# Output projection of a cross-attention stage in bursts, with the next layer's normalisation moved into it

## The reference, cut to what matters

```python
def _attend(q, k, v):                         # 16 heads of 64; once for 77 text keys, once for 179 image keys
    sim = jnp.einsum('bihd,bjhd->bhij', q, k) * SCALE
    attn = jax.nn.softmax(sim, axis=-1)
    out = jnp.einsum('bhij,bjhd->bihd', attn, v)
...
out = out + IMG_SCALE * out_ip
return out @ Wo + bo                          # 1024 -> 512: the output projection
...
def act_qdq(x):                               # in _L0_ffn_ref, on its input and on every intermediate tensor
    qmax = 2.0 ** (ACT_BITS - 1) - 1.0        # 32767
    scale = jnp.maximum(jnp.max(jnp.abs(x)) / qmax, 1e-12)
    return jnp.clip(jnp.round(x / scale), -qmax - 1.0, qmax) * scale
...
x = x + _L0_xattn_ref(_layernorm(x, axis=-1), ctx_1024, L0_xattn_Wq, ...)
x = x + _L0_ffn_ref(_layernorm(x, axis=-1), L0_ffn_w_gate, L0_ffn_w_up, L0_ffn_w_down)
```

## Time and profile before

| | us |
|---|---|
| median of the runs (lowest, highest) | 3874.53 (3872.53, 3882.94) |
| the profiled execution, its own time | 3887.41 |
| its span, first to last instruction | 3885.8 |
| TensorE busy | 3228.7 (83%) |
| VectorE, ScalarE, GpSimd busy | 2026.4, 1531.7, 709.6 |
| mean granted clock of TensorE | 0.915 |

### The profile page before, as it was taken

One profiled execution on the slowest core, in us unless ns is written; L12 is line 12 of the kernel. 1 busy time (PEld: TensorE's weight loads), 2 busy tenths in 40 slices (PEclk: granted clock), 3 DMA queues, 4 the chain that ended last, 5 costly groups with the idle time before them and its releaser, 6 DMA issues. The chain is left out here.

```text
span 3885.8 us, 52312 instructions
## 1 busy us (share of the span) xinstructions
PE 3228.7 (83%) x17152; PEld 2765.4 (71%) x17152; DVE 2026.4 (52%) x3424; ACT 1531.7 (39%) x2927; POOL 709.6 (18%) x1093
## 2 busy tenths in 40 slices
PE   7999799999999717998991069968881999999998
PEld 6989788888888606886880058836761877777776
DVE  3343377767677564556899955416763222222221
ACT  2222266666666423335777856503332111111110
POOL 0000277777777410000000000000000000000000
PEclk9999899999999858999995579978995999999999
DMA  6666544444444233445665544313324000100000
GB/s 173 170 206 188 176 141 140 134 130 140 137 139 124 78 103 133 160 141 171 210 205 165 164 140 162 135 57 109 120 89 121 22 33 33 33 30 31 20 31 16
DMA packets 330783, 457.31 MB, mean 118 GB/s; under 512 B 55616, under 2 KB 199232, under 8 KB 327946
## 3 DMA queue, kind: packets, MB, share of 16 engines
q1 hardware_dynamic: 316660, 438.94, 36.3%
q0 software_dynamic: 3328, 14.68, 1.0%
q10 hardware_dynamic: 10592, 1.04, 0.2%
HBM read 276.29 MB, written 144.70 MB: 108 GB/s over the span
## 5 line engine op out<-in xcount | busy, mean ns | idle before, releaser
L2254 DVE SCALAR_TENSOR_TENSOR lf_hT<-lf_hb,lf_hT 128x512 fp32r<-128x512 f32 x128 | 88.6, 692 | 638.4 <-ACT lf_hT L2312 637.1
L2312 ACT ACTIVATE lf_hT<-lf_hb 128x512 fp32r<-128x512 f32 x128 | 76.6, 599 | 699.2 <-PE lf_py L179 641.6
L177 PE MATMUL dn_py<-qf_wd,dn_om 128*128 128x512 f32 x384 | 150.5, 392 | 220.4 <-DVE dn_om L1641 220.4
L694 POOL TENSOR_TENSOR at_prob<-at_prob,at_rec 128x308 f32<-128x308 f32 (+1 forms) x256 | 261.5, 1044 | 230.8 <-DVE at_rec L731 230.8
L775 ACT ACTIVATE at_prob<-at_sc,at_nm 128x77 f32<-128x77 f32 (+1 forms) x1024 | 292.8, 381 | 3.7 <-DVE at_nm L718 3.6
L718 DVE TENSOR_REDUCE at_nm<-at_sc 128x4 f32<-128x308 f32 (+1 forms) x256 | 164.9, 686 | 178.4 <-PE at_sc L822 178.4
L177 PEld LDWEIGHTS dn_py<-qf_wd,dn_om 128*128 128x128 f32 x384 | 72.6, 189 | 235.8 <-issue 220.8
L788 ACT ACTIVATE at_pT<-at_tp 128x1024 fp32r<-128x1024 f32 x128 | 131.6, 1028 | 258.3 <-PE at_tp L832 258.2
L178 PE MATMUL lf_hb<-lf_xT,lf_w 128*128 128x512 f32 x512 | 203.7, 398 | 5.2 <-issue 5.2
L177 PE MATMUL lf_hb<-lf_xT,lf_w 128*128 128x512 f32 x512 | 205.1, 401 | 0.0
L179 PE MATMUL lf_hb<-lf_xT,lf_w 128*128 128x512 f32 x512 | 203.4, 397 | 0.0
(11 more groups left out here) (304 smaller groups left out, 9458.6 us busy)
## 6 DMA issues: line engine op xcount, KB each, us to landing
at_kr<-k_rows SPq DMA_DIRECT2D x256, 128.0 KB, 2.9
at_qs<-at_qst SPq DMA_DIRECT2D x512, 64.0 KB, 2.0
raw_gate<-pg_stage SPq DMA_DIRECT2D x96, 256.0 KB, 2.0
pu_rg<-raw_gate SPq DMA_DIRECT2D x96, 256.0 KB, 2.9
raw_up<-pu_stage SPq DMA_DIRECT2D x96, 256.0 KB, 2.0
om_raw<-raw_up SPq DMA_DIRECT2D x48, 512.0 KB, 3.8
dn_raw<-raw_up SPq DMA_DIRECT2D x48, 512.0 KB, 3.8
xn_parts<-pr_xturned SPq DMA_DIRECT2D x32, 512.0 KB, 3.8
```

The source lines that it names most:

```text
L177: pe.matmul(out, lh, rh, start=start, stop=False, **kw)
L694: ins = pool.tensor_tensor(prob[:, i, :, lo:hi], prob[:, i, :, lo:hi], rec[:, z, g, :].unsqueeze(2).broadcast_to([P, 2 * NTE, hi - lo]), A ...
L2254: dve.scalar_tensor_tensor(hT[:, i, 1, :], hb[i][:], 0.0, hT[:, i, 0, :].bitcast(F32), ALU.max, ALU.subtract).then_inc(h_done, 1)
```

## The change

- **Bursts.** `out_part` with its 4 pieces is replaced by `project_out`: all 24 matmuls of a tile at the end of one step in four (`out_tile(s)`, steps 12, 16, 20, ...). The buffers of the attention outputs grow from 10 to 13 pairs for it.
- **Normalisation in the pair stage.** For the tile projected in step s: VectorE adds it to the residual in step s+1, ahead of the second `totals`, and takes its statistics at the step's end; GpSimd makes the deviation and the shift at the start of step s+2; ScalarE normalises into `xn` in step s+3, ahead of `high_parts`; in step s+4 TensorE turns the tile in `pj` before its scores, ScalarE copies it out before its turned probabilities, VectorE takes the row maxima; in step s+5 SyncE stores it as float32 into `x1_turned`. The next `project_out` waits for `o_taken`, that copy.
- **Buffers and lags.** `place_values` works on pair s-3 instead of s-2 (`LAG_P` 2 to 3), in 2 buffers instead of 3 (`NVP`). The loops run 4 steps longer.
- **The pass is gone.** `normalize_all` and `normalized_rows` are deleted. The scale is worked out at the end of the pair stage. The gate projection loads the float32 rows (1 MB a chunk instead of 0.5 MB), ScalarE turns them into integers first and then makes the high part, and SyncE stores the integers to `xq` for the up projection.

The diff, cut to its core:

```diff
@@ attend_pairs
-    LAG_T, LAG_V, LEAD_Q, LAG_P = 3, 4, 3, 2
+    LAG_T, LAG_V, LEAD_Q, LAG_P = 3, 4, 3, 3
-    NPR, NY, NO, NQ, NQS, NK, NKR, NVP = 4, 3, 10, 4, 2, 4, 4, 3
-    OPIECES = 4
-    FIRST, LAST = -LEAD_Q, N + LAG_O
+    NPR, NY, NO, NQ, NQS, NK, NKR, NVP = 4, 3, 13, 4, 2, 4, 4, 2
+    EVERY = NPAIR // NTE
+    FIRST, LAST = -LEAD_Q, N + LAG_O + 4
...
-        def out_piece(s):
+        def out_tile(s):
             i = s - LAG_O
-            return (i // NPAIR, i % NPAIR // OPIECES, i % OPIECES) if 0 <= i < NPAIR * B else None
+            return (i // NPAIR, i % NPAIR // EVERY) if 0 <= i < NPAIR * B and i % EVERY == EVERY - 1 else None
@@ SyncE
+                def store_turned(b, t):
+                    n = NTE * b + t
+                    sp.wait_ge(o_taken, n + 1)
+                    lo = b % NB * S + t * P
+                    sp.dma_start(xt_d[b // NB].rearrange("p (k n) -> p k n", k=KD)[:, :, lo:lo + P], xt[:, n % 2]).then_inc(xt_stored[n % 2], 16)
...
-                    done = s - LAG_O - NPAIR - 1
+                    done = s - LAG_O - NPAIR - 3
...
+                    if out_tile(s - 5):
+                        store_turned(*out_tile(s - 5))
@@ GpSimd
+                def deviation(b, t):
+                    steps = Count(pool, norm_steps, 3 * (NTE * b + t))
+                    wait_alone(pool, mv_ready, NTE * b + t + 1, spacer_p)
+                    steps.done(pool.tensor_scalar(var[:], mv[:, 1:2], EPS, None, ALU.add))
+                    steps.wait()
+                    if b + t:
+                        pool.wait_ge(xn_ready, NTE * b + t)
+                    steps.done(pool.tensor_tensor(rstd[:], var[:], neghalf[:, 0:1], ALU.pow))
+                    steps.wait()
+                    steps.done(pool.tensor_tensor(shift[:], mv[:, 0:1], rstd[:], ALU.mult))
+                    wait_alone(pool, norm_steps, steps.base + steps.n, spacer_p)
+                    pool.tensor_scalar(shift[:], shift[:], -1.0, None, ALU.mult).then_inc(shift_ready, 1)
...
-                for s in range(-LEAD_KL, N + LAG_P):
+                for s in range(-LEAD_KL, LAST + 1):
+                    if out_tile(s - 2):
+                        deviation(*out_tile(s - 2))
                     if 0 <= s - LAG_P < N:
                         place_values(s - LAG_P, 0)
...
+                pool.wait_ge(row_max, 1)
+                pool.partition_all_reduce(big[:, 0:1], mx_row[:], P, RMAX).then_inc(all_max, 1)
@@ VectorE
+                def statistics(b, t):
+                    n = NTE * b + t
+                    dve.wait_ge(y_done, n + 1)
+                    dve.bn_stats(st[:], y[:, b % NY, t, :]).then_inc(stat_done, 1)
+                    wait_alone(dve, stat_done, n + 1, spacer_d)
+                    if n:
+                        dve.wait_ge(shift_ready, n)
+                    dve.bn_aggr(mv[:], st[:]).then_inc(mv_ready, 1)
+                def row_maximum(b, t):
+                    n = NTE * b + t
+                    dve.wait_ge(xn_ready, n + 1)
+                    dve.tensor_reduce(mx[:, n:n + 1], xn[:], AX_X, ALU.max, apply_absolute_value=True).then_inc(mx_done, 1)
...
                         totals(s - 1, 0)
+                    if out_tile(s - 4):
+                        row_maximum(*out_tile(s - 4))
                     if 0 <= s - LAG_T < N:
                         turned_low(s - LAG_T)
+                    if out_tile(s - 1):
+                        output(*out_tile(s - 1))
                     if 0 <= s - 1 < N:
                         totals(s - 1, 1)
                         reciprocals(s - 1)
                     if s < N + LAG_V:
                         low_parts(s)
-                    piece = out_piece(s - 1)
-                    if piece and piece[2] == OPIECES - 1:
-                        output(*piece[:2])
+                    if out_tile(s - 1):
+                        statistics(*out_tile(s - 1))
@@ ScalarE
+                def normalized(b, t):
+                    n = NTE * b + t
+                    wait_alone(act, shift_ready, n + 1, spacer_a)
+                    if n:
+                        act.wait_ge(o_full, n)
+                        act.wait_ge(mx_done, n)
+                    act.activation(xn[:], y[:, b % NY, t, :], ACT.Identity, bias=shift[:], scale=rstd[:]).then_inc(xn_ready, 1)
...
+                    if out_tile(s - 4):
+                        turned_output(*out_tile(s - 4))
                     if 0 <= s - LAG_T < N:
                         turned_high(s - LAG_T)
...
                         keys_high(s + LEAD_KH)
-                    high_parts(s)
+                    if out_tile(s - 3):
+                        normalized(*out_tile(s - 3))
+                    if s < N + LAG_V:
+                        high_parts(s)
@@ TensorE
+                def turn_output(b, t):
+                    pe.wait_ge(xn_ready, NTE * b + t + 1)
+                    for k in range(KD):
+                        ins = pe.transpose(pj[:, k * P:(k + 1) * P], xn[:, k * P:(k + 1) * P], ident[:])
+                    ins.then_inc(o_full, 1)
+                def project_out(b, t):
+                    if b + t:
+                        pe.wait_ge(o_taken, NTE * b + t)
+                    if t == 0:
+                        pe.wait_ge(vq_done, v_count(NPAIR * b + NPAIR - 1))
+                    for p in range(NPAIR):
...
+                    ins.then_inc(out_full, 1)
                 for s in range(FIRST, LAST + 1):
+                    if out_tile(s - 4):
+                        turn_output(*out_tile(s - 4))
...
-                    piece = out_piece(s)
-                    if piece:
-                        out_part(*piece)
+                    if out_tile(s):
+                        project_out(*out_tile(s))
@@ quantized_ffn
-                    normalize_all(nc, x1, xq, big, scal, ident, neghalf)
-                    project(nc, "pg", xq, wg, raw_gate, big, S_G, I_G, scal, meanwhile=lambda ph: Meanwhile(
+                    project(nc, "pg", xq, wg, raw_gate, big, S_G, I_G, scal, turned=xt_d, meanwhile=lambda ph: Meanwhile(
@@ project, ScalarE
                     act.wait_ge(xi_ready[par], 16 * half + 16)
+                    if turned is not None:
+                        act.wait_ge(x_lo, c + 1)
+                        act.wait_ge(xq_stored[par], 16 * half + 16)
+                        act.activation(xi[:, par], xf[:, par], ACT.Copy, scale=scal[:, I_X:I_X + 1]).then_inc(x_int, 1)
+                        act.wait_ge(x_int, c + 3)
```

More of the change, by code:

```diff
@@ L226, in cross_attention @@
         project_context(nc, a, x_in, ctx_in, xn_d, k_d, v_d, wq, wo, ident, neghalf)
[L227 removed]
+        attend_pairs(nc, a, x_in, xn_d, k_d, v_d, x1, xt_d, wq, wo, big, scal, ident, neghalf)
 def project_context(nc, a, x_in, ctx_in, xn_d, k_d, v_d, first, second, ident, neghalf):
@@ L538, in _, with attend_pairs @@
                         turn(n)
-def attend_pairs(nc, a, x_in, xn_d, k_d, v_d, x1, wq, wo, ident):
+def attend_pairs(nc, a, x_in, xn_d, k_d, v_d, x1, xt_d, wq, wo, big, scal, ident, neghalf):
     SEG = [(0, TEXT), (TEXT, S)]
@@ L573, in attend_pairs @@
         pj = ph.ps("pj", [P, D])
+        xn = ph.sb("xn", [P, D])
+        xt = ph.sb("xt", [P, 2, KD, P])
+        st = ph.sb("st", [P, 6])
+        mv = ph.sb("mv", [P, 2])
+        var = ph.sb("var", [P, 1])
+        rstd = ph.sb("rstd", [P, 1])
+        shift = ph.sb("shift", [P, 1])
+        mx = ph.sb("mx", [P, B * NTE])
+        mx_row = ph.sb("mx_row", [P, 1])
+        stat_done, mv_ready, norm_steps, shift_ready, xn_ready, mx_done, o_full, o_taken = (
+            ph.sem(n) for n in ("stat_done", "mv_ready", "norm_steps", "shift_ready", "xn_ready", "mx_done", "o_full", "o_taken"))
+        xt_stored = [ph.sem(f"xt_stored{i}") for i in range(2)]
+        row_max, all_max, settled, spacer_d, spacer_p, spacer_a = (
+            ph.sem(n) for n in ("row_max", "all_max", "settled", "spacer_d", "spacer_p", "spacer_a"))
         cleared, bo_ready = ph.sem("cleared"), ph.sem("bo_ready")
@@ L799, in high_parts @@
                     ins.then_inc(vq_hi, 1)
-                for s in range(FIRST, N + LAG_V):
+                for s in range(FIRST, LAST + 1):
+                    if out_tile(s - 4):
+                        turned_output(*out_tile(s - 4))
                     if 0 <= s - LAG_T < N:
@@ L1272, in project @@
-def project(nc, name, xq, w, raw, big, scale, inverse, scal, raw_gate=None, gate=None, meanwhile=None):
+def project(nc, name, xq, w, raw, big, scale, inverse, scal, raw_gate=None, gate=None, turned=None, meanwhile=None):
     NBANK = 4
@@ L1293, in project @@
         xi_ready = [ph.sem(f"xi_ready{i}") for i in range(2)]
-        x_hi, x_lo = ph.sem("x_hi"), ph.sem("x_lo")
+        x_int, x_hi, x_lo = ph.sem("x_int"), ph.sem("x_hi"), ph.sem("x_lo")
+        xq_stored = [ph.sem(f"xq_stored{i}") for i in range(2)]
         r_full, r_copied, max_done = ph.sem("r_full"), ph.sem("r_copied"), ph.sem("max_done")
```

(21 more changed lines are left out.)

159 lines of the change are left out of this document (21 added, 138 removed).

## The result

| | before | after |
|---|---|---|
| median of the runs (lowest, highest), us | 3878.31 (3872.53, 3882.94), 4 runs | 3817.47 (3811.49, 3821.6), 4 runs |
| the profiled execution, its own time | 3887.41 | 3818.55 |
| its span | 3885.8 | 3816.9 |
| mean granted clock of TensorE | 0.915 | 0.923 |

The ratio is 0.9837, 95% interval 0.9823 to 0.9852. The forecast was 3818 us. The median before now has a fourth run in it; the forecast started from 3874.5, the median of the first three, so it stood for 56 us less, where the medians differ by 61.

The account below looks back on a forecast made before the run. TensorE was taken to bound the pair stage and gate projection, the deleted stage being serial time. Removal -89, tiles +17, ends +16 gave -56 us, from 3874.5 to 3818 us; own range 3790 to 3840, overall 3775 to 3855.

Parts of the forecast that it names:

- The removal: Before the gate projection: the 90.5 us stage goes, first gate matmul near 1408.6 instead of 1497.49, -89 us.
- The tile: Pair stage, steps 13 to 125: 26.35 us without bias, 28.15 with; mean 27.9 against 27.3, +17 us.
- The four transposes: TensorE in the pair stage: four added transposes a tile, 4 x 0.099 = 0.40 us.
- The head and the last steps: Pair stage ends: first twelve steps +2 us, as the first bias delays the placing; light steps 125 to 127, -4.
- The tail: After the last scores: delayed placing 3.4, two more projection pieces 2.8, uncovered serial chain 8 and 3.5; +18 us.
- beside the last store: End of the pair stage: the maximum over rows and its reduction run beside the last store.
- The price of the power: GpSimd's deviation: the one-column power takes 0.41 us, between 0.20 and 1.04; the chain 1.45 us.
- Rival D: GpSimd's one-column power costs 1.04 us as before: +20 us, or +30 with the SP queue; 3843 us, chance 0.10.
- B: Pair stage: queues and slack absorb GpSimd's and VectorE's lateness, tile 24.7 + 0.36, 78 us less; 3740 us, chance 0.12.
- C: Gate projection: ScalarE's double conversion holds the banks, +27 us; 3845 us, chance 0.07.
- E: Pair stage: two or three half-clock stretches a tile; at 2.5 a tile +99 us, 3917 us; chance 0.05.
- One sign to look for: Pair stage, every second tile: TensorE waits at `at_vq` on GpSimd's `at_vs`, 2.5 to 3.5 us.

Follow-up runs that it names:

- e_bias4: Changed kernel with GpSimd adding the bias in step 4 of 8 (the burst step) instead of step 5; 3766.57 us.
- e_devlate: Changed kernel with GpSimd's deviation behind the placing of the values instead of ahead of it; 3790.6 us.
- e_bursts_lag3: Kernel before with the bursts alone, plus values placed for pair s-3 in 2 buffers; separate pass over x1 kept; 3829.13 us.
- e_bursts: Kernel before with only `project_out` in place of the four pieces, old lag of 2, separate pass over x1 kept; 3799.96 us.
- e_noreduce: Changed kernel with the reduction over partitions at the pair stage's end replaced by a plain GpSimd copy; 3822.21 us in one run.
- e_inburst: Changed kernel with bias, statistics, deviation and normalisation moved to the time of the next burst, transposes eight steps behind their own burst; 3734.43 us.
- before_again: Kernel before, unedited, run again for a second trace; 3875.8 us in one run.
- after_again: Changed kernel, unedited, run again for the spread and a second trace; 3817.78 us, ratio to before 0.9824.

## Why the prediction was right, and where it was not

**The removal.** Predicted -89 us. From the first dequantising instruction of VectorE to the first gate matmul it is 144.8 us before (1352.7 to 1497.5) and 55.9 after: -88.9. Conversion 2.00 for 1.91; the load issued at 1427.43 is used at 1432.23, 4.8 for 5.2. Right.

**The tile.** Without the bias 4.69 + 4.91 + 6.13 + 10.25 = 25.98 us, predicted 26.35. With it, at full clock, 28.44, predicted 28.15. Half-clock stretches came in nine of the 14 tiles with the bias and cost some 2.05 us where they came, which is 1.3 for each of the 14 and 0.66 for the mean tile; predicted 0.68, from nine in ten at 1.5 each. That these two agree is luck: they came less often than forecast and cost more. So is part of the rest: in the tile without the bias the forecast had 0.5 us for a wait of the transposes on ScalarE's normalisation, and the profile lists no such wait in 600:1200. The mean of the 28 tiles from step 13 to 125 is 27.87, predicted 27.9. The mechanism is shown too: e_bias4 takes the bias out of GpSimd's late step and the long wait is gone; e_devlate takes the deviation from ahead of the placing and the wait halves. In the forecast this term holds two things that run against each other: the bursts and the lag bring the tile from 27.39 to 25.39 (e_bursts_lag3), and the normalisation brings it back to 27.87. The sum against before came out at +13.5 instead of +17, since before's own tile over these steps was 27.39, while the forecast worked with 27.3.

The four transposes cost what the row said. In the tile without the bias the values start at 904.65 and take 2.95, and the transposes start behind them:

```profile
907.59 0.66 PE L944 MATMUL at_pj<-ident,at_xn 128*128 128x128 f32 x4
908.00 1.20 PE L908 MATMUL at_sc<-at_ks,at_qs 128*128 128x256 f32 x8
```

They put 0.41 us into the path. The figure of the Trainium skill ("TensorE: Matmul & The Clock Gate", Part 4), about 275 ns for one transpose of 128x128 in bf16, would by estimate give 1.1 us if each had to end before the next. As the time of one instruction the trace agrees with it, for float32: 273 ns is the median of the 128 at L944. But in a stream the next work starts some 0.1 us after each, and that is what they cost.

**The head and the last steps.** Predicted +2 and -4. The placing was late in step 7 as said (6.64 us instead of 4.70), but a wait on a DMA of 2.55 us with a half-clock stretch, in step 8 of before, did not come back: -3.2 from step 0 to 13. That is luck of this pair of profiles, and no effect of the change: in the second profile of the kernel before this wait is 1.05 us and no stretch follows, in e_bursts it is 3.44, and between the second profiles these steps differ by +1.8, as forecast. Steps 125 to 127: -6.

**The tail is the mis-sized term.** Predicted +18, measured +26.5 (+28.2 between the second profiles): from the last scores to the dequantisation it is 38.7 us before and 65.2 after. The chain between the last two bursts takes 5.7 us from the end of the addition (1352.57) to the next burst (1358.24), not 4.0, and stands in the path twice; the transposes take 1.11 at half clock, not 0.4; the last burst takes 7.50 us (1358.24 to 1365.74) and not the 5.6 of full clock. The prediction put the reduction "beside the last store". It starts 3.68 us after the row maximum that it reads has ended, and VectorE's wait of 4.09 for it stands there, but e_noreduce shows that only 0.8 us of it counts. The phase change behind the stage takes 10.6 us (1372.08 to 1382.70), where it took 8.8 before (1343.9 to 1352.7). Together 2 x 1.7 + 1.9 + 1.8 = 7.1 of the 8.5 us; the other 1.4 is not told apart. e_bursts_lag3, with 46.4 us for the same distance, puts 7.7 of the 26.5 on the bursts and the lag and 18.8 on the normalisation. The forecast counted the links of the tail at full clock, but TensorE is idle between them, and of the clock the transposes and the burst were granted this (columns as in the earlier trace rows):

```profile
1356.40:1358.20 1.80, 1.11 (x4) 0.71 (x4) 0.69 (x1) 0.60 (x1) 0.00 (x0) 0.50 0.00 0
1358.20:1365.80 7.60, 7.50 (x24) 5.71 (x24) 0.02 (x1) 0.00 (x0) 0.00 (x0) 0.75 0.12 35
```

The errors cancel: 13.5 - 3.2 - 6 + 26.5 = +31 in the stage, where the forecast had +17 + 16 = +33, so the stage and the removal give -58, for -56. Between the second profiles it is -50. So the mechanism of the tile and the removal was right, and the closeness of 3817.5 to 3818 is luck to some us. (The distance between the spans of the two profiles, 69, has 11 of the untouched stages in it.)

**The price of the power** on one column is 0.57 us, between the 0.41 chosen and the 1.04 of the earlier trace rows; the whole chain is 1.58, not 1.45. Rival D, which had it at 1.04, fell: 32 x 0.16 = 5 us were to be lost at most, and in the stage neither ScalarE nor SyncE has a listed wait on the landing of a store. (D's 3843 us is the middle of its two ends; with the +30 of its text it is 3848.)

**One slip in the working.** In the earlier trace rows the last low part ends 0.95 us after the reciprocal, so from 5.95 it ends at 6.90 and not at the 6.76 of the forecast, 0.14 us a tile. The first light step behind a burst took 4.91 us, +0.21 where the forecast had +0.36, so the slip decided nothing.

**The other rivals.** B (the bursts are absorbed, 3740) did not come: slack in front of the normalisation didn't help what stood behind it. e_inburst shows that the same work can be absorbed, 3734 us, once it stands in the step in which GpSimd and VectorE have time; so B was wrong as a forecast of this order, and about right (25.2 us a tile, for 24.7 + 0.36) for another. C (the gate projection gives back) fell: TensorE is busy for 275.9 us of it, 274.9 before, with ScalarE 96 us busy for 85. E (the clock) fell: between steps 13 and 125 half-clock stretches come with the waits of 3.1 to 3.5 us alone, and cost 0.66 a tile, not the 1.6 at which the gain would be gone.

**One sign to look for was named wrongly.** The prediction expected a wait on GpSimd's `at_vs` in the view. The view says "issue", and only the order of time (placing ends at 933.03, TensorE starts at 933.13) shows who it was. That it is GpSimd is shown by the runs: e_bias4 and e_devlate change GpSimd's list alone, and the one takes the long wait away and the other halves it; e_bursts_lag3, which shortens the lag between GpSimd and TensorE, brings a wait there about.

## What to carry to other kernels

When one engine gets its work in bursts, the others have their slack while the burst runs and little elsewhere; side jobs belong there in each list, behind what the busy engine needs next. Here the kernel took 3817 us with these jobs behind the burst and 3734 with them beside the next one. Deleting a pass is worth its length only if its work finds such slack: in the order first built, nearly all of the 88 us of the pass were paid back in the stage that took its work. A lag between producer and consumer is slack: before shortening it to free a buffer, sum up what the producer's engine has ahead of it in its worst step. A stage's end is to be counted link by link with the clock that TensorE has when it is idle between links.

## What the runs showed of the hardware

- Between steps 13 and 125, TensorE's granted clock fell at 12 and 10 of 28 waits of 2.13 us (before, before_again), for 3.4 us each; at 9, 8 and 11 of 14 waits of 3.1 to 3.5 us (after, after_again, e_noreduce), for 3.4 or 6.8 us; and at none of the waits of 0.3 to 1.61 us (after, e_bias4, e_devlate, e_bursts_lag3, e_inburst).
- The power (`ALU.pow`) on GpSimd took 1.04 us for four columns and 0.57 for one, while the small products beside it stayed at 0.19 to 0.20: by these two, 0.41 and 0.16 for each column.
- The reduction over partitions takes 0.38 us. At the end of the pair stage it starts 5.61 to 5.74 us after GpSimd's last ordinary instruction in five profiles, and 3.68 to 3.81 us after the row maximum that it reads has ended; the copy of e_noreduce starts 0.07 us after it. In the kernel before, GpSimd's idle time ahead of it is as long, but there the row maximum ended only 0.14 us before the reduction started, so it waited for VectorE, as the view says. Both fit a preparation of some 5.6 us that starts when the ordinary work ends; no run shows what it is.

```profile
1460.91 0.16 DVE L1267 TENSOR_REDUCE nr_mx_row<-nr_mx 128x1 f32<-128x8 f32 x1
1461.21 0.38 POOL L1231 PARTITION_ALL_REDUCE qf_big<-nr_mx_row  x1 [5.78 <-DVE nr_mx_row L1267]
```

After the change:

```profile
1369.05 0.24 POOL L728 TENSOR_SCALAR at_shift<-at_shift 128x1 f32<-128x1 f32 x1 [0.20 <-POOL at_shift L726]
1374.90 0.38 POOL L755 PARTITION_ALL_REDUCE big<-at_mx_row  x1 [5.61 <-issue]
```
